# A 32-batch decoder block on one core: GpSimd powers in place of Newton steps for the roots of three norms, and a new order of the steps

## What is computed

```python
def _layernorm(x, eps=1e-05):
    return (x - mean(x)) / sqrt(var(x) + eps)
...
x = x + _L0_attn_ref(_layernorm(x), Wq, Wk, Wv, Wff, bff)               # self attention, 16 heads
x = x + _L0_xattn_ref(ctx_1024, ctx_1024, _layernorm(x), ...)           # cross attention over 750 rows
x = x + _L0_ffn_ref(_layernorm(x), ...)
# _L0_ffn_ref(h): scores over 2048 keys through a router of 48, top 8 of them, softmax, sum of 8 gathered rows
variance = ((h - mean(h)) ** 2).mean(-1)
log_var = log1p(variance)
normalized_var = log_var / (log_var.mean() + 1e-06)                      # the mean goes over all batches
gate = sigmoid(gate_w1 * clip(normalized_var * 0.5 + sigmoid(learned) * 2.5, 0, 5) + gate_bias)
out = h + gate[..., None] * agg
```

## Time and profile before

| | |
|---|---|
| median of 3 runs | 2811.0 us (2810.16 to 2812.33) |
| profiled execution, first to last instruction | 2786.2 us |
| instructions | 56938 |
| PE busy | 2556.4 us, 92% of the span |
| DVE busy | 2146.0 us, 77% |
| ACT busy | 1431.3 us, 51% |
| POOL busy | 683.1 us, 25% |
| granted clock of PE, mean | 0.971 of full |
| chain that ended last | PE 74%, DVE 8%, ACT 7%, issue 7%, DMA 2%, POOL 1% |

### The profile page before, as it was taken

One profiled execution on the slowest core, in us unless ns is written; L12 is line 12 of the kernel. 1 busy time (PEld: TensorE's weight loads), 2 busy tenths in 40 slices (PEclk: granted clock), 3 DMA queues, 4 the chain that ended last, 5 costly groups with the idle time before them and its releaser, 6 DMA issues.

```text
span 2786.2 us, 56938 instructions
## 1 busy us (share of the span) xinstructions
PE 2556.4 (92%) x19090; PEld 2104.0 (76%) x19090; DVE 2146.0 (77%) x4207; ACT 1431.3 (51%) x4247; POOL 683.1 (25%) x650
## 2 busy tenths in 40 slices
PE   6899999999999999999999999999999999999730
PEld 4578878887888788878887888778888887788520
DVE  5456888888888888888888888888888888887552
ACT  2345554555555545555555455555554555555252
POOL 0001222222222222222222222222222222222254
PEclk9899999999999999999999999999999999999955
DMA  5223354454544444444444445444445454444799
GB/s 189 53 80 80 107 132 121 128 137 130 133 121 112 130 125 123 138 131 131 128 111 128 131 113 138 131 131 131 115 126 134 106 139 130 132 130 111 202 205 178
DMA packets 131542, 358.87 MB, mean 129 GB/s; under 512 B 21906, under 2 KB 26514, under 8 KB 123267
## 3 DMA queue, kind: packets, MB, share of 16 engines
q0 software_dynamic: 63520, 160.60, 24.4%
q1 hardware_dynamic: 63188, 192.15, 23.6%
q10 hardware_dynamic: 4784, 5.46, 0.6%
HBM read 316.37 MB, written 41.78 MB: 129 GB/s over the span
## 4 chain that ended last, share of the span: by engine, by line
PE 74%; DVE 8%; ACT 7%; issue 7%; DMA 2%; POOL 1%; DVEq 0%; ACTq 0%; POOLq 0%; SPq 0%
PE psX L1144 43%; PE psA L1144 13%; PE psA L1153 5%; PE psF L1144 4%; PE psA L1210 4%; DVE top L999 3%; PE psA L1233 2%; ACT paT L640 2%; PE psX L1153 2%; ACT sc L640 1%; DMA vg<-in_L_ffn_aux_values,idx 1%; ACT xT_hi L663 1%; DVE xmax L948 1%; PE psF L1153 1%; DVE idx L1002 1%
## 5 line engine op out<-in xcount | busy, mean ns | idle before, releaser
L589 POOL DMA_INDIRECT vg<-in_L_ffn_aux_values,idx x512 | 491.7, 960 | 1550.5 <-DVE agg L1028 1053.8
L684 ACT ACTIVATE pa<-psA,nmax 112x224 f32<-112x224 f32 x1024 | 444.6, 450 | 197.8 <-DVE nmax L917 194.5
L917 DVE TENSOR_REDUCE nmax<-psA 112x4 f32<-112x896 f32 x256 | 267.1, 1085 | 100.9 <-PE psA L1210 100.9
L1144 PE MATMUL psX<-big,gT 128*112 128x375 f32 x1024 | 333.4, 478 | 0.6 <-ACT gT L711 0.6
L1028 DVE SCALAR_TENSOR_TENSOR agg<-vg,wt,agg 112x512 f32<-112x512 f32 x406 | 303.8, 748 | 9.2
L1144 PE MATMUL psX<-pT,cx 125*128 125x224 f32 x1536 | 299.1, 355 | 0.0
L1144 PEld LDWEIGHTS psX<-pT,cx 125*128 125x128 f32 x1536 | 288.0, 190 | 4.0 <-issue 0.3
L932 DVE TENSOR_TENSOR pa<-pa,rsum 112x896 f32<-112x896 f32 x256 | 279.4, 1091 | 8.8
L1144 PEld LDWEIGHTS psX<-big,gT 128*112 128x112 f32 x1024 | 175.2, 176 | 126.0 <-issue 0.9
L1153 PE MATMUL psA<-ident,pa 112*112 112x112 f32 x2048 | 227.2, 262 | 19.5 <-DVE oT_lo L895 19.4
L640 ACT COPY paT<-psA 112x448 f32<-112x448 f32 x512 | 237.2, 560 | 11.4 <-PE psA L1153 9.4
(11 more groups left out here) (220 smaller groups left out, 5957.0 us busy)
## 6 DMA issues: line engine op xcount, KB each, us to landing
big<-in_ctx_t SPq DMA_DIRECT2D x32, 1500.0 KB, 8.1
cx<-in_ctx SPq DMA_DIRECT2D x32, 1344.0 KB
xa<-in_x SPq DMA_DIRECT2D x64, 224.0 KB
centered<-in_x_t SPq DMA_DIRECT2D x32, 448.0 KB, 4.6
x<-in_L_attn_bff POOLq DMA_DIRECT2D x32, 448.0 KB, 5.7
x<-cb_scratch POOLq DMA_DIRECT2D x32, 448.0 KB, 5.9
x<-in_x SPq DMA_DIRECT2D x31, 448.0 KB
out<-x SPq DMA_DIRECT2D x30, 448.0 KB, 3.1
```

The lines of the kernel that those rows point to most:

```text
L589: pool.indirect_dma_start(vg[:, c % SLOTS, k, :], None, aux_values, bass.IndirectOffsetOnAxis(ap=idx[:, t, n:n + 1], axis=0))\
L684: last = nc.scalar.activation(pa[:, t, h, :], psA[0:R, h, t * S:(t + 1) * S], ACT.Exp, bias=nmax[:, k % 2, h, t:t + 1], accum_out=rsum[:, ...
L917: nc.vector.tensor_reduce(nmax[:, k % 2, h:h + 2, :], psA[0:R, h:h + 2, 0:T * S].rearrange("p h (t s) -> p h t s", t=T), AX_X, ALU.max, ne ...
L1144: last = nc.tensor.matmul(dst, stationary, moving, start=n == 0, stop=n == len(pairs) - 1)
```

## The change

1. The seed and the three Newton rounds of each norm go from DVE. In their place stands a step "root" on POOL, `norm_root`: one `tensor_tensor` with the power of -0.5 on [112, 2]. The part of a norm up to `ve` is a step of its own ("stat"), on DVE, and the norming waits for `rooted`. The store of the moments of norm 1 waits for POOL's root.
2. The variance of the normed rows is no longer measured. It is worked out as variance times root times root by two `tensor_tensor` on POOL, behind `add_base`.
3. X enter is two steps of one bank each.
4. `ORDER`, `FIRST` and `LAST` are new. Two lines of `ORDER` stand in the diff below.

```diff
-    ("N", "center", 0), ("F", "route", 0), ("A", "mix", 0), ("X", "prob", 0), ("A", "prob", 1), ("F", "learn", 0),
+    ("N", "center", 0), ("F", "route", 0), ("X", "prob", 0), ("A", "mix", 0), ("G", "sum", 4), ("A", "prob", 1),
...
-FIRST = (("N", "norm", 0), ("N", "spread", 0), ("W", "mean", 0), ("N", "center", 0), ("W", "split", 0),
+FIRST = (("N", "stat", 0), ("N", "root", 0), ("N", "spread", 0), ("W", "mean", 0), ("N", "center", 0), ("W", "split", 0),
...
-N_STEPS, A_STEPS, X_STEPS, F_STEPS, G_STEPS = 13, 8, 15, 18, 12
+N_STEPS, A_STEPS, X_STEPS, F_STEPS, G_STEPS = 3, 8, 5, 5, 12
...
             def store_moments(b, _):
-                sp.wait_ge(steps["N"], N_STEPS * (b + 1))
+                sp.wait_ge(rooted["N"], b + 1)
...
+            nc.gpsimd.memset(power[:, :], -0.5).then_inc(const_step, 1)
...
                 nc.gpsimd.tensor_tensor(dst[:, :, :], x2[:, :, :], xnf[:, :, :], ALU.add).then_inc(base_ready, 1)
+                nc.gpsimd.tensor_tensor(var_part[:, :], mv["F"][:, :, 1], rstd["F"][:, :], ALU.mult).then_inc(var_step, 1)
+                pool.wait_ge(var_step, b + 1)
+                nc.gpsimd.tensor_tensor(columns(var_all, b), var_part[:, :], rstd["F"][:, :], ALU.mult).then_inc(var_taken, 1)
+
+            def norm_root(s):
+                def step(b, _):
+                    pool.wait_ge(steps[s], per_batch[s] * b + MOMENTS)
+                    if s == "N":
+                        wait(pool, moments_stored, 16 * b)
+                    apart(pool)
+                    nc.gpsimd.tensor_tensor(rstd[s][:, :], ve[s][:, :], power[:, :], ALU.pow).then_inc(rooted[s], 1)
+                return step
...
             def log_var(*_):
-                act.wait_ge(steps["F"], F_STEPS * B - T)
+                act.wait_ge(var_taken, B)
...
-            def statistics(s, b, src, rstd):
+            def statistics(s, b, src):
...
+                if s == "F":
+                    wait(dve, var_taken, b)
...
                 mark(s, nc.vector.tensor_scalar(ve[s][:, :], mv[s][:, :, 1], EPS, None, ALU.add))
-                settle(s, b)
-
-                if s == "N":
-                    wait(dve, moments_stored, 16 * b)
-                mark(s, nc.vector.tensor_scalar(rstd.bitcast(I32), ve[s][:, :].bitcast(I32), -0.5, RSQRT_SEED,
-                                                ALU.mult, ALU.add))
-                for _ in range(3):
-                    settle(s, b)
-                    mark(s, nc.vector.scalar_tensor_tensor(tmp[s][:, :], rstd, -0.5, ve[s][:, :], ALU.mult, ALU.mult))
...
             def norm(s, b, src, dst, normed):
-                statistics(s, b, src, rstd[s][:, :])
+                dve.wait_ge(rooted[s], b + 1)
...
                 norm("F", b, x2, xnf, x2_normed)
-                dve.wait_ge(x2_normed, b + 1)
-                for t in range(T):
-                    last = nc.vector.bn_stats(stats["F"][:, t, :], xnf[:, t, :])
...
```

More of the change, by code:

```diff
@@ L28 @@
 F32R = mybir.dt.float32r
-I32 = mybir.dt.int32
 U32 = mybir.dt.uint32
@@ L231, in build @@
         rstd = {s: sb(f"rstd_{s}", [R, T]) for s in "NXF"}
-        tmp = {s: sb(f"tmp_{s}", [R, T]) for s in "NXF"}
+        power = sb("power", [R, T])
+        var_part = sb("var_part", [R, T])
         var_all = sb("var_all", [R, B * T])
@@ L538, in _ @@
                           ("W", "cb"): first_cxT, ("W", "gb"): first_ctx,
-                          ("X", "score"): next_cxT, ("X", "mix"): next_ctx, ("N", "norm"): store_moments,
+                          ("X", "score"): next_cxT, ("X", "mix"): next_ctx, ("N", "root"): store_moments,
                           ("N", "spread"): spread_moments, ("N", "center"): next_xt, ("X", "enter"): entered, ("R", "load"): next_xr,
@@ L935, in share, with x_enter @@
                 assert k < NB - 1 or count["A"] == A_STEPS
[L937 to L943 removed]
+            def x_enter(b, t):
+                if t == 0:
+                    dve.wait_ge(xr_biased, 16 * (b + 1))
+                j = FILL["X", "enter", t]
+                wait_full(dve, "X", j, b)
+                nc.vector.tensor_tensor(x1[:, t, :], bank("X", j)[0:R, :], x1[:, t, :], ALU.add)\
+                    .then_inc(drained["X"][j % banks["X"]], 1)
             def x_maxima(b, t):
```

77 lines of the change are left out of this document (33 added, 44 removed), and 44 rows, old and new, of tables (LAST, ORDER).

## The result

The changed kernel took 2906.2 us (2902.4 to 2907.7, 4 runs), the kernel before beside it 2810.7 us (2810.2 to 2812.3): a ratio of 1.0333, with an interval of 1.0321 to 1.0346. I had forecast 2827 us and a range that ended at 2850. The direction is right, the size is not: 95 us instead of 16.

What follows compares the result with a forecast made beforehand. An iteration was taken to cost PE's matmuls plus PE's waits. Profiled 2786.2 + 10.1 - 7.5 + 13.0 + 0.5 = 2802.3 us; with the 24.8 us around it, 2827 us, range 2798 to 2850.

Steps and rivals of the forecast that it cites:

- The head: Start of the run: POOL's first root waits for the small constants, N center at 35.7 instead of 25.56: +10.1 us.
- Iteration 0: PE's 3.50 us wait at 93.62 goes (-3.5) and most of the low clock behind it (-4.0): -7.5 us.
- The steady iteration: The `pT` copy now stands ahead of `oT_lo` on DVE, delaying PE's fill 0.42 us: +13.0 us over 31 iterations.
- The power: POOL's root on 112x2, taken as 0.5 us; up to about 0.8 costs nothing, beyond it each iteration loses the excess.
- In steady state I cost that at nothing: DVE's relief of 8.4 us per batch, 270 us over the run, gains nothing, as DVE's critical work waits for PE.
- The ending: ACT's `Ln` behind POOL's last addition comes later by the two products added behind that addition: +0.5 us.
- the third rival: A dear power on POOL delays DVE's maxima: at 1.5 us +22, 2849 us; at 2.35 us 2875; chance 0.13.
- The swap is free: X prob 0 ahead of A mix 0 costs nothing at `oT_lo`, so the 13 us vanish: 2814 us; chance 0.13.
- It ends faster: PE's wait on `oT_lo` goes altogether through DVE's relief: -15.8 in place of +13.0, 2798 us; chance 0.15.
- The power is dear: POOL's root over about 0.8 us makes DVE's maxima late each iteration: 2849 us at 1.5, 2875 at 2.35; chance 0.13.
- The head is absorbed: Loads later in iteration 0, not yet awaited through this chain, absorb part of the head's loss: 2817 us; chance 0.08.
- The first power pays for its code: POOL's first power in the head waits once for its code: 2828 us at 1.28, 2833 at some 6; chance 0.04.

Runs made afterwards that it cites:

- the second set: Runs beside the kernel before (2784.6 us): changed kernel unaltered 1.0074, its roots as Newton on DVE 1.0429, POOL's roots in the old order 1.0028, joined kernel 0.9993.
- joined kernel: Changed kernel with first root ahead of the small constants' wait, A mix 0 ahead of X prob 0, G sums 4 and 5 at old places: 0.9993 of before.
- the candidate: POOL's roots in the old ORDER, norm 1's stat, root and spread ahead of A score 1, first root ahead of the constants' wait: 0.9981 and 0.9986 of before.
- the doubled power: Changed kernel with every root worked out twice by POOL, one behind the other with a semaphore between: 1.0442 of the kernel before.
- four edits: Four single edits of the changed kernel (gathers late, A mix 0 first, G sums back, root first): 1.0089, 1.0083, 1.0091, 1.0065 of before.

## Why the prediction was right or wrong

**The direction and the terms, where semaphores were on time.** On the chip of the second set the changed kernel took 1.0074 of the kernel before, some 21 us; the sum had been 16. The nearness is partly luck, since its terms missed in both directions. They are, from the times of the `xT_lo` of the two traces (the forecast column has the 13.0 us of the sum shared out over the 31 iterations that they stand for):

| term | forecast, us | measured, us |
|---|---|---|
| head, to N center | +10.1 | +6.5 |
| iteration 0, from N center on, and the low clock behind its wait | -7.5 | -6.2 |
| one more iteration | +0.4 | +0.3 |
| all up to the `xT_lo` of batch 3 | +3.0 | +0.7 |
| a steady iteration, 27 of them | +0.42 | +0.77 |
| the ending, with the last three iterations | +1.8 | -2.6 |

- *The head.* The mechanism is right: the first root waits for the last small constant, and stands ahead of nothing else.

```profile
23.91 0.73 POOL L600 TENSOR_TENSOR rstd_N<-ve_N,power 112x2 f32<-112x2 f32 x1 [19.97 <-DMA gbc<-in_L_ffn_gate_bias]
```

  N center started at 32.08 us, not 35.7. The step that failed took ACT's issue of that constant at 23.34 us for fixed. In the new trace it is issued at 20.52 and lands 3.2 us later: one of ACT's issues ahead of it took 1.06 us instead of 4.04. Store and spread took 7.4 us, near the 8.0 of the earlier trace rows, where I had taken them from. With the root moved ahead of that wait, N center starts at 26.84 us.
- *Iteration 0.* The mechanism is right. The 3.5 us wait of PE went, and most of the low clock with it; part stayed (0.84 in the window 93 to 104 us). The mis-sized part is the clock: in the window of the earlier trace rows PE is now busy for 8.31 us at 0.83, and by the sum's own reckoning (estimate) that loses 1.4 us where 0.50 lost 4.2, so 2.8 us came back and not 4.0. With the 3.5 that makes 6.3, against 6.2 measured: N center of batch 1 comes 8.9 us earlier behind the head, and 2.7 of these are gone by the next one. This stretch differs between executions, though: the kernel before with gathers late, run twice, took 78.9 and 82.7 us from the second `xT_lo` to the third.
- *The steady iteration.* The place is right: PE's wait at the fourth fill of prob 1 is 1.09 us instead of 0.51 in every iteration, 0.58 more, where I took 0.42. The mis-sized step is the copy's length: I took the distance of other starts, 0.31 to 0.42, but from `pT` to `oT_lo` it is 0.54 (1003.47 to 1004.01 on DVE), nearer to the 0.50 that the row itself reads and outside the bounds.

  The other 0.2 us are a term that the sum did not have. They stay in the joined kernel of the second set (79.58 against 79.38 us), and no group of PE's waits carries them, because that list leaves out waits of under 0.15 us. They stand behind qk 3, where PE's first product of X score 1 needs the bank that ACT frees with its exponentials of X score 0. In the changed kernel of the second set (timelines of DVE, ACT and PE):

```profile
882.43 0.93 DVE L952 TENSOR_REDUCE xmax<-psX 112x1 f32<-112x750 f32 x1
883.40 0.57 ACT L742 ACTIVATE nx<-psX,xmax 112x375 f32<-112x375 f32 x1 [1.46 <-DVE xmax L952]
884.12 0.57 PE L1148 MATMUL psX<-big,gT 128*112 128x375 f32 x1
```

  and with the roots in the old order:

```profile
880.41 0.94 DVE L951 TENSOR_REDUCE xmax<-psX 112x1 f32<-112x750 f32 x1 [2.05 <-PE psX L1147]
881.38 0.57 ACT L741 ACTIVATE nx<-psX,xmax 112x375 f32<-112x375 f32 x1 [1.25 <-DVE xmax L951]
882.81 0.48 PE L1147 MATMUL psX<-big,gT 128*112 128x375 f32 x1
```

  There DVE's maxima `xmax` wait for PE. In the new order G sum 3 and A share 1 stand ahead of them on DVE, they start when DVE comes free, and ACT is late with the bank: its semaphore is raised 0.04 us before PE starts, in the old order 0.76. From the last product of qk 3 to the second one of X score 1 it takes 0.65 us instead of 0.43, in all 27 steady iterations. That A share 1 is the step that does it is argued from the timeline; no run moves it alone.
- *The power.* 0.73 us for 0.5, under the threshold of about 0.8, and with hardly any slack left; in the old order it costs nothing (79.38 us), and doubled it makes an iteration longer behind maxima 1, as the third rival described.
- *"In steady state I cost that at nothing."* True of the old order, shown by the roots in the old order. In the new order the relief is what keeps PE from waiting at qk 3: with Newton on DVE the iteration is 83.9 us, 3.8 more. I treated relief and order as separate edits, and they are not: the order spends the relief.
- *The ending.* Forecast +0.5 and three iterations' share, measured -2.6 from the `xT_lo` of batch 30 to the end. That stretch took 388.9 and 387.3 us in two executions of one text and 392.4 in the kernel before, so part of it may be scatter; it was not followed further.

**The 65 to 75 us more.** The step that failed is one that the sum holds at nothing without a reason: the new places of the G sums. The prediction counts gathers in one sentence only, as about 0.95 us of POOL each ahead of norm 3's root. I walked through when they would start, but only asked what waits for POOL and for their data. In the new order four gathers come one behind another across score 2, and on chips of one kind the semaphores that PE raises meanwhile come 3.1 to 3.2 us late. From there the chain is the ordinary one (maxima 2, top 8, `pa`, PE at prob 2, clock), and it costs 3 us of an iteration (83.10 against 80.19 us with two gathers moved). Nothing in the trace of before shows it: that execution has lags of 0.27 to 0.30 us although gathers run across its scores too, and its span of 2786.2 us is that of a chip of the first kind. One sign was there: 24.8 us between the span and the median. I called it what lies around the span. It was a hint that the timed chip and the profiled one differ, by 0.8%, and that the trace might not show what bounds the kernel where it is timed.

**The rivals.** "The swap is free" is out (0.58 us). "It ends faster" is out: with the relief and the old order the wait on `oT_lo` stays at 0.50 us, and the candidate's 0.998 comes from the head and iteration 0, not from that wait. "The power is dear" is right in its mechanism, as the doubled power shows, and had the wrong side of the threshold: 0.73 lies just under it. "The head is absorbed" has nothing for it: with the root moved ahead of the wait, N center comes 5.2 us earlier and the `xT_lo` of batch 3 8.3 us. "The first power pays for its code" is out (0.73 us). No rival named the gathers.

## What to carry to other kernels

A new order of one engine's work changes which instants of other engines coincide. When a step issues DMAs, ask not only when its data land but what is raised, on any engine, while it issues. And before four edits are believed to have cured something, run the unaltered kernel beside them on the same chip.

When one part of a change relieves an engine and another re-orders the work, cost them together: here the relief alone was worth nothing in a steady iteration, the order without the relief cost 4.3%, and both together 0.7%.

A gap between a profiled span and the timed median is a finding, not a constant to add: here it was 24.8 us, where the 19 later profiled runs have 2 us. And a delay of PE that repeats can lie below what a list of waits counts; comparing starts over the same sequence of matmuls finds it.

## What the runs showed of the hardware that I had not expected

- **Late semaphores beside gathers.** On the three chips where the kernel before takes 2806 to 2811 us, the semaphores of PE's scores are raised late while POOL issues indirect DMAs: 1.00 us behind PE's last matmul where the first gather of a run starts 0.36 us ahead of it, 3.07 to 3.2 us where two have been issued and a third starts with it, 0.27 to 0.31 us where none is being issued any more or yet. PE itself goes on with its next matmuls meanwhile. On three of the four chips where the kernel before takes 2783 to 2785 us the same texts ran, and show 0.27 us with the same gathers at the same distances; on the fourth other texts did, with the same result. What differs between the chips, and by what path one engine's DMAs hold back another's semaphores, is not shown: the runs that move gathers move their issue and their transfers together. The first comparison's chip is counted with the three by its time and its lags.
- **The price of a power.** 0.70 to 0.74 us for 224 elements, against 0.21 us for a product of the same size and 2.37 us for an addition of 112x1024. The Trainium skill, GPSIMD Engine Reference, section 3.1 (Elementwise), counts two-input elementwise work at about twice VectorE's time; DVE's 0.16 us for a product by that rule gives an estimate of about 0.33 us, which holds roughly for the product and not for the power. The Trainium skill, section 2.1 (Instruction dispatch) of the same page, has some 6 us for the first call to a freshly loaded function; the first power here took 0.73 us like the rest, and none of these runs shows such a start.
